# Variance product issued ahead of centring in twelve norms, routes two chunks ahead in the trees, earlier feed-forward entries, nine table loads left out

## The reference, cut to what matters

```python
def _ln(x, g, b):
    m = x.mean(-1, keepdims=True)
    v = x.var(-1, keepdims=True)
    return (x - m) * jax.lax.rsqrt(v + 1e-05) * g + b
```

```python
for level in range(8):
    n = 2 ** level
    g = gate[:, n - 1:2 * n - 1]
    lp = lp * leaf_factors(g)      # (1 - g, g), spread over the level's 2n subtrees
out = lp @ leaf_values @ Wout_w
```

## Time and profile before

| | us |
|---|---|
| three timed runs, median | 1332.65 |
| lowest and highest of them | 1327.83, 1334.56 |
| the profiled execution, its own time | 1330.96 |
| its span, first to last instruction | 1329.2 |
| around the span | 1.8 |

### The profile page before, as it was taken

One profiled execution on the slowest core, in us unless ns is written; L12 is line 12 of the kernel. 1 busy time (PEld: TensorE's weight loads), 2 busy tenths in 40 slices (PEclk: granted clock), 3 DMA queues, 4 the chain that ended last, 5 costly groups with the idle time before them and its releaser, 6 DMA issues.

```text
span 1329.2 us, 20391 instructions
## 1 busy us (share of the span) xinstructions
PE 1173.4 (88%) x7508; PEld 645.8 (49%) x7516; DVE 924.3 (70%) x1508; ACT 847.3 (64%) x1333; POOL 206.4 (16%) x313
## 2 busy tenths in 40 slices
PE   8997899999999798799997798798888887788776
PEld 3333344444444353377763353376666664443244
DVE  3877688777777575467773564588998993557655
ACT  6867655556556644745675437577887776557674
POOL 1000000000000000000000000276877773000000
PEclk9999999999999899989998899788999999899899
DMA  6000112112111000000000000000000000000002
GB/s 161 1 0 0 44 55 69 63 64 62 58 63 48 0 1 9 1 1 2 2 1 0 1 0 8 1 2 2 2 2 2 15 2 9 0 1 0 0 0 64
DMA packets 26076, 27.16 MB, mean 20 GB/s; under 512 B 3885, under 2 KB 17024, under 8 KB 25984
## 3 DMA queue, kind: packets, MB, share of 16 engines
q1 hardware_dynamic: 25938, 25.92, 6.5%
q10 hardware_dynamic: 46, 0.01, 0.0%
HBM read 23.30 MB, written 2.62 MB: 19 GB/s over the span
## 4 chain that ended last, share of the span: by engine, by line
PE 60%; DVE 17%; ACT 14%; issue 7%; POOL 1%; DMA 0%; DVEq 0%; ACTq 0%
PE psum L571 8%; PE psum L582 8%; PE psum L70 4%; PE psum L574 4%; PE psum L789 4%; PE psum L816 3%; PE psum L79 3%; ACT ln_std L95 3%; ACT ln_std L97 3%; PE psum L1723 3%; PE psum L1399 2%; DVE arena L1233 2%; DVE arena L1899 2%; DVE N L1908 2%; PE psum L1167 2%
## 5 line engine op out<-in xcount | busy, mean ns | idle before, releaser
L606 ACT ACTIVATE arena<-psum 128x512 f32<-128x512 f32 x128 | 69.5, 594 | 114.5 <-PE psum L571 114.5
L571 PE MATMUL psum<-arena,weights 128*128 128x512 f32 x256 | 122.3, 600 | 1.8 <-DVE N L112 1.1
L582 PE MATMUL psum<-arena,weights 128*128 128x512 f32 x256 | 120.4, 592 | 0.0
L79 PE MATMUL psum<-ln_sq,mean 128*128 128x512 f32 x192 | 97.1, 606 | 1.5 <-ACT ln_sq L87 1.4
L469 DVE SCALAR_TENSOR_TENSOR arena<-diff,vecs,N 128x512 f32<-128x512 f32 x128 | 95.1, 746 | 0.0
L1819 ACT ACTIVATE N<-N 128x1024 f32<-128x1024 f32 x64 | 67.7, 1058 | 35.0 <-DVE N L1908 34.2
L1733 PE MATMUL psum<-ident,N 128*128 128x128 f32 x512 | 75.4, 294 | 12.6 <-POOL N L1872 11.4
L530 DVE SCALAR_TENSOR_TENSOR arena<-arena,psum 128x512 f32<-128x512 f32 x64 | 43.9, 686 | 60.7 <-PE psum L582 60.7
L1723 PE MATMUL psum<-arena 32*128 32x128 f32 x1024 | 80.0, 298 | 4.8 <-ACT arena L1787 4.8
L106 DVE TENSOR_TENSOR Y<-psum,ln_std 128x512 f32<-128x512 f32 x48 | 33.2, 692 | 73.2 <-ACT ln_std L97 73.2
L1723 PEld LDWEIGHTS psum<-arena 32*128 32x128 f32 x1024 | 67.1, 199 | 32.2 <-issue 16.2
(11 more groups left out here) (325 smaller groups left out, 2489.7 us busy)
## 6 DMA issues: line engine op xcount, KB each, us to landing
arena<-tw_rows SPq DMA_DIRECT2D x64, 256.0 KB, 3.0
out_dram<-arena SPq DMA_DIRECT2D x8, 256.0 KB, 3.6
arena<-in_L_attn_a_x_dram SPq DMA_DIRECT2D x3, 512.0 KB, 6.4
weights<-in_L_attn_a_eWk_dram SPq DMA_DIRECT2D x1, 1024.0 KB, 5.8
arena<-in_L_attn_a_x_dram SPq DMA_DIRECT2D x2, 256.0 KB, 3.2
weights<-in_L_attn_a_eWr_dram SPq DMA_DIRECT2D x1, 512.0 KB, 9.6
tw_rows<-arena SPq DMA_DIRECT2D x2, 128.0 KB, 2.6
tw_rows<-arena SPq DMA_DIRECT2D x1, 256.0 KB, 3.7
```

Of the source, the lines that this page charges most:

```text
L79: nc.tensor.matmul(k.bank[W + (c - 2) % vary][:], k.mean[:], k.ln_sq[:, (c - 2) % W, :], start=True, stop=True).then_inc(k.ln_var, 1)
L571: op = nc.tensor.matmul(k.bank[2 * (n % 2) + h][:], k.eWk[:, e, h * P:(h + 1) * P], mixed[:, n % 4, 0, :], start=True, stop=True)
L582: op = nc.tensor.matmul(k.bank[4 + n % 2][:], k.eWv[:, e, h, :], ks[:, (2 * (n % 2) + h) * CH:(2 * (n % 2) + h + 1) * CH], start=(h == 0), ...
L606: op = nc.scalar.activation(kr[:, h * CH:(h + 1) * CH], k.bank[2 * (n % 2) + h][:], ACT.Relu)
```

## The change

Four things are altered; what is computed stays the same.

1. In every norm TensorE's list becomes variance `c-2`, then centring `c` (then the feed). Norms 10 and 12 use two PSUM banks for the variance in place of three, as norms 1 and 11 did already.
2. At the end of norms 5 and 8 the next norm's first centring and first square are issued early (`ahead`): the square stands between the exponential of chunk 6 and the logarithm of chunk 7.
3. In the feed-forward part the fills of `u` and the cast move into the norm's feed (chunks 0, 1 and 6), and the first three hidden products wait only for the scale steps of chunks 4, 5 and 6.
4. In the tree the routes and gates run two chunks ahead of the turns and not one, with other banks for it, and the first route waits for no scale step. A table load is written only where the table differs from the one loaded last (`activations`). The store at the end uses other banks, and the weights' preparation in norm 10 moves from chunks 5 and 7 to 6 and 8.

```diff
+def activations(act, k, table):
+
+    if k.table != table:
+        k.table = table
+        act.preload_act_table_set(table)
...
+    def center(self, pe, c):
+        if self.again("center", c):
+            return
+        k = self.k
+        if self.enter is not None:
+            self.enter(pe, c)
+        pe.wait_ge(k.ln_out, self.n0 + c + 1)
+        self.nc.tensor.matmul(k.bank[c % W][:], k.center[:], self.src(c), start=True, stop=True).then_inc(k.ln_centered, 1)
...
     @block.tensor
     def _(pe):
         for c in range(NCH + 2):
+            if c >= 2:
+                norm.variance(pe, c - 2)
             if c < NCH:
-                if enter is not None:
-                    enter(pe, c)
-                pe.wait_ge(k.ln_out, n0 + c + 1)
-                nc.tensor.matmul(k.bank[c % W][:], k.center[:], src(c), start=True, stop=True).then_inc(k.ln_centered, 1)
+                norm.center(pe, c)
             if feed is not None:
                 feed[0](pe, c)
-            if c >= 2:
-                pe.wait_ge(k.ln_squared, n0 + c - 1)
-                if clear is not None:
-                    clear(pe, c - 2)
-                if c - 2 >= vary:
-                    pe.wait_ge(k.ln_logs, n0 + c - 1 - vary)
-                nc.tensor.matmul(k.bank[W + (c - 2) % vary][:], k.mean[:], k.ln_sq[:, (c - 2) % W, :], start=True, stop=True).then_inc(k.ln_var, 1)
...
+def ahead(after):
+
+    def first(pe, c):
+        if c == NCH + 1:
+            after.center(pe, 0)
+
+    def turned(act, c):
+        if c == NCH - 2:
+            after.square(act, 0)
+
...
     def begin(dve, c):
+        if c < 2:
+            nc.vector.memset(u[c][3 * DM:P, :], 0.0).then_inc(k.ff_up, 1)
+            dve.wait_ge(k.ff_up, 2 * call + c + 1)
+            nc.vector.memset(u[c][3 * DM:3 * DM + 1, :], 1.0).then_inc(k.ff_hot0, 1)
+        if c == 6 and call == 0:
+            dve.wait_ge(k.ff_const, 2 + NP)
+            dve.wait_ge(k.ff_spread, 5)
+            nc.vector.tensor_copy(k.spread16[:], k.spread).then_inc(k.ff_spread16, 1)
...
-        for c in range(2):
-            nc.vector.memset(u[c][3 * DM:P, :], 0.0).then_inc(k.ff_up, 1)
-            dve.wait_ge(k.ff_up, 2 * call + c + 1)
-            nc.vector.memset(u[c][3 * DM:3 * DM + 1, :], 1.0).then_inc(k.ff_hot0, 1)
-        if call == 0:
-            dve.wait_ge(k.ff_const, 2 + NP)
-            dve.wait_ge(k.ff_spread, 5)
-            nc.vector.tensor_copy(k.spread16[:], k.spread).then_inc(k.ff_spread16, 1)
...
-            pe.wait_ge(k.ff_spread16, 1)
             pe.wait_ge(k.ff_const, 2 + NP)
-        pe.wait_ge(k.ff_hot0, 4 * call + 4)
-        pe.wait_ge(k.ln_out, normed)
...
             for j in range(GR):
+                if first:
+                    pe.wait_ge(k.ln_out, normed - 3 + j)
                 pe.wait_ge(k.ff_hid, g * 3 + (j + 1))
                 nc.tensor.matmul(k.bank[j][:], k.W1[:, j, :], xm[c], start=True, stop=True).then_inc(k.ff_h, 1)
...
+                hidden(it, c, first and c == 0)
+                if first and c == 0:
+                    pe.wait_ge(k.ln_out, normed)
+                    pe.wait_ge(k.ff_hot0, 4 * call + 4)
+                else:
+                    if first and call == 0:
+                        pe.wait_ge(k.ff_spread16, 1)
                     spread(*before)
                 scores(it, c)
...
-        if c == 5:
+        if c == 6:
...
-        if c == 7:
+        if c == 8:
...
-    nodes = [k.pair[c].rearrange("p (t m) -> p t m", m=M) for c in range(2)]
-    turned, summed = k.pair[2], (k.bank[6], k.bank[7])
+    nodes = [k.pair[c].rearrange("p (t m) -> p t m", m=M) for c in (3, 0)]
+    turned, summed = k.pair[2], (k.bank[2], k.bank[3])
...
         pe.wait_ge(k.tw_ready, 3)
         route(0)
+        pe.wait_ge(k.ln_out, normed - 2)
+        route(1)
+        pe.wait_ge(k.ln_out, normed)
         for n in range(NCH):
-            if n + 1 < NCH:
-                route(n + 1)
+            if n + 2 < NCH:
+                route(n + 2)
             turn(n)
             if n >= 1:
                 leaves(n - 1)
...
         gate(0)
+        gate(1)
         for n in range(NCH):
-            if n + 1 < NCH:
-                gate(n + 1)
+            if n + 2 < NCH:
+                gate(n + 2)
             turn(n)
```

More of the change, by code:

```diff
@@ L63, in _, with layernorm @@
+def layernorm(k, block, norm, feed=None):
+    k.ln_done, k.ln_logged = norm.n0 + NCH + PRIMED["ln_out"], norm.n0 + NCH
     @block.tensor
@@ L1145, in tree_weights, with tree @@
     return turn, keep
-def tree(nc, k, block, call, out=None):
+def tree(nc, k, block, call, after):
     TI, M, DEPTH = CH // P, 256, 8
@@ L1248, in _, with stage_tree @@
         add(NCH - 1)
-def stage_tree(nc, k, block, a, enter, clear, out=None):
+def stage_tree(nc, k, block, a, norms):
+    first, after = norms
     call = k.tr_calls
     k.tr_calls += 1
-    X, Y = (lambda c: plain(k.X, c)), (lambda c: plain(k.Y, c))
-    layernorm(nc, k, block, X, Y, enter=enter, clear=clear, feed=tree_weights(nc, k, a) if call == 0 else None)
-    tree(nc, k, block, call)
+    layernorm(k, block, first, tree_weights(nc, k, a) if call == 0 else None)
+    tree(nc, k, block, call, after)
 def favor_loads(nc, k, block, a):
@@ L2192, in build @@
         with nc.Block() as block:
-            feed = load(nc, k, block, a)
+            loaded, *feed = load(nc, k, block, a)
+            norms = all_norms(nc, k, loaded)
             with ExitStack() as own:
```

257 lines of the change are left out of this document (150 added, 107 removed).

## The result

| | before | changed |
|---|---|---|
| median of four runs, us | 1331.93 | 1293.24 |
| lowest and highest | 1327.83, 1334.56 | 1289.76, 1298.22 |
| the profiled execution, its own time | 1330.96 | 1289.76 |
| its span | 1329.2 | 1288.0 |
| instructions named ACT_TABLE_LOAD | 21 | 12 |

The ratio is 0.9715 (0.9668 to 0.9762). A later group of runs on another chip gave 0.970 (0.9659 to 0.9741). The forecast was 1292.

What follows compares the result with a forecast made beforehand. No engine bounds throughout; runnable instructions stand behind waiting ones in each engine's list. Nine terms sum to 40.3 us: 1330.96 - 40.3 = 1290.7, and with the runs' median 1.7 higher, 1292; range 1283 to 1303.

Steps and rivals of the forecast that it cites:

- norm 10 with the first tree: Norm 10 and tree 1 together: 14.9 us gained at full clock, 9.7 with the old low-clock stretches; 13.5 taken.
- Norms 1 and 2: The first two norms together: 1.3 us gained.
- The norm's loop: In a norm, a turn of two chunks falls from 4.21 to 3.83 us; logarithm 0 starts 0.48 later.
- The net 0.28 for a plain norm: Plain norm: two turns gain 0.38 us each, 0.76, less logarithm 0 starting 0.48 later, net 0.28.
- Norms 5 into 6: From norm 5 through norm 6, load removed and square early: 2.5 us gained, between 2.2 and 3.4.
- Entries: Feed-forward entries, hidden products and fills in the norm's shadow: 7.0 us gained at the first, 6.2 at the second.
- Tree: Turn 0 to turn 7 falls to 27.6 us; gains 8.2 and 7.2 in the two trees at full clock.
- the gate ahead of the copy eats the gain: Tree rival: gate n+2 delays copy n and the leaves, 15 us of gain lost, 1307 us; chance 0.06.
- closes a chain: Tree rival, slower: ScalarE's list makes levels n+1 wait for add n-1, about 1362 us; chance 0.02.
- my bookkeeping: Instruction lists laid side by side with durations; for norm 10, last scale step 4.7 to 6.1 us earlier, turn 0 6.7.
- Four of the loads taken out are exposed: Of the nine removed table loads, four cost time, at most 5.2 us at 1.28 each; the other five 0.
- The rival that it stays or moves: TensorE's low clock stays or moves to new places: gains only 32.3 us, so 1300 us; chance 0.16.

Runs made afterwards that it cites:

- e2: The changed kernel with TensorE's list in every norm again centring, feed, variance; 1297.01 us, ratio 0.9722.
- e3: The changed kernel with feed-forward fills and cast behind the norm again and the first hidden product waiting for them and the whole norm; 1297.22 us, ratio 0.9734.
- e6: The changed kernel with ScalarE's square c+2 behind exponential c, not ahead of logarithm c, in every norm; 1265.83 us, ratio 0.9521.
- e7: The changed kernel without the early centring and square at the end of norms 5 and 8; 1291.63 us, ratio 0.9718.
- e4: The changed kernel with all 21 table loads written as before, not 12; 1294.24 us, ratio 0.9713.
- e10: e6 plus two unused 128x512 products in TensorE's idle places in each feed-forward part; 1259.56 us, ratio 0.9473.
- e1: The changed kernel with routes and gates in both trees one chunk ahead again, new banks kept; 1307.32 us, ratio 0.9791.

## Why the prediction was right

- *The sum.* The nine terms gave 44.58 and not 40.3, and the stages between them, which I had put at nothing, lost 3.37. That the total of 41.21 came so near is in part luck. Two terms lay above what I took: norm 10 with the first tree (15.43 for 13.5) and the second entry (7.63 for 6.2). Norms 1 and 2 (1.07) start with a stretch that differs by 1.4 us among executions, so that term is not tested finely.
- *The norm's loop.* 4.21 became 3.84 (3.83 forecast), and logarithm 0 came 4.22 after centring 0 and not 3.64 + 0.48 = 4.12. The net 0.28 for a plain norm was too much: e2 shows 0.15 in norm 12 and nothing in norms 4 and 7, where the fills also cost 0.2 (e3). The swap's 7.4 us come from the norms with more in their lists and the joints: 3.0 in norms 5 and 6, 2.9 around norm 10, 1.1 in norms 8 and 9. What I took as given, square 2 ahead of logarithm 0, turned out to be worth more than the swap on TensorE (e6, 25 us).
- *Norms 5 into 6.* 3.39 and not 2.5, the top of the range, since the clock did not drop there: the granted clock over norm 6 is 1.00, and was 0.92 from 538 to 560 us before. Norm 6's loop took 13.97 to 13.98 us in each of the kernels that are the same there. The early square delays norm 5's last logarithm by 0.47 (0.48 forecast), and VectorE covers nearly all of it, as I had said (e7). The joint wins 0.54.
- *Entries.* 6.92 and 7.63 against 7.0 and 6.2. (In the working, 453.2 against 460.58 is 7.4 and not 7.3.) From norm 7's last logarithm the second entry won 6.03, within its bounds; the rest of the 7.63 is norm 7. Its start, from centring 0 to logarithm 0, took 5.77 before, with the granted clock 0.64, and 4.72 after, with 0.82. It took 6.27 in e4 and e7, so that 1.05 belongs to the execution and not to the edit. The statement behind the term, that at this entry the idle time goes and with it the low clock, was only half right. A smaller idle time of 1.47 and 1.20 us stayed. In the first part the low clock moved from the first hidden group to the second, which took 2.74 before and takes 4.44 now, and the body as a whole gave back 1.36. In the second part the second group ran at the low clock before as well (4.44 and 4.54). e10 shows that the idle time is what brings it: filled, the group takes 2.74.
- *Tree.* 27.61 in both trees against 27.6, at full clock, where they took 35.81 and 34.82. Copy 5 stands behind gate 7 until 1146.15, and what that costs is 0.60 us of waiting ahead of turn 6. So the rivals in which the gate ahead of the copy eats the gain, or closes a chain, fell. e1 gives the size: 15.8 for 8.2 + 7.2.
- *Norm 10.* From its first centring to turn 0 it took 32.69 and takes 25.45, so 7.24 for the 6.7 of my bookkeeping, and its granted clock is 1.00 and was 0.91. e2 gives 3.1 of this to the variance ahead of the centring. How the other 4 or so divide between the later preparation of the weights, the earlier first route, the second bank and the clock, no run shows.
- *Loads.* "Four of the loads taken out are exposed" was five (e4), 4.6 us. It did not touch the sum, since norm 12 was worked out as a whole (0.6) and its turn 0 came 0.56 earlier. The Trainium skill (ScalarE: Activation LUTs, What ACT_TABLE_LOAD costs) adds 1.38 us for draining to a switch to another set. No row here shows it. Both rows of e4, where the set stays, show 1.29 from the load's start to the next square's start. The load at 449.91 in the changed kernel, which does change the set, starts 0.02 after the last exponential's end and has tanh 1.30 behind it. The measurement decides: there is no such drain here.
- *The clock.* The rival that it stays or moves was forecast to cost 8 at worst, and in part it came true: both second hidden groups run at the low clock. By e10 that costs 1.69 us in each part, 3.4 in all. The Trainium skill (TensorE: Matmul & The Clock Gate, What's actually happening) says that the throttled state is the default and activity releases it. e10 agrees: with 1.7 us of unused products the granted clock from 440 to 447 us is 1.00, where the same place has 0.72 in the changed kernel.

## What to carry to other kernels

When engines run their lists in order, look in the rows for an instruction whose inputs are long there and that stands behind one that waits, and after each swap look again one engine further, because the swap on TensorE was worth 7 us and the one on ScalarE that it made possible 25. Look where the swap pays, too: in the plain norms it gave 0.15 us or nothing, and nearly all of it came from norms whose lists hold more. Read a loop's gain as intervals in the steady part and at the start of it apart: here the start (1.35 us in each of twelve norms) was the larger. An idle time of TensorE costs twice where the clock falls behind it, so price the work behind it at half the rate, and try unused products where nothing real can be moved in. Then look at the stage and not at the clock alone: in the feed-forward parts they won 1.7 us each, in the segments and Favor no gain in time is shown.

## What the runs showed of the hardware that I had not expected

- Two idle times of TensorE of 0.95 to 1.47 and 1.20 us, with only small products between them, were followed by the low clock in 16 of 16 cases (3.73 to 5.29 us for six records of 128x512, where 2.74 is the full rate). With one product of 0.86 us in each gap the same group took 2.74 in four of four. A single idle time of 3.31 to 6.24 us ahead of the first group was followed by 4.28 to 5.49 us for that group in six of six cases; the second group, 1.20 us of idle time before it, was then at the full rate in two of them.
- A load of the table that is in place costs 1.28 us like any other: it is not skipped. None of the loads whose rows are shown here, to the same set or to another, is followed by a further wait.
- Stages that no edit touched differ by up to 7 us from one profiled execution to the next, with low-clock stretches in other places each time, while the norms between their logarithms and the trees between their turns repeat to 0.02 us.
